# Curvature stage: where the mixed square, the cross product and the numerator stand in each engine's queue

## What is computed

```python
def step(u, _):
    ux, uy, uxx, uxy, uyy = _derivs(u)          # Sobel stencils, each clipped to -10..10
    g2 = ux * ux + uy * uy
    denK = jnp.maximum(1.0 + g2, EPS)
    K = jnp.clip((uxx * uyy - uxy * uxy) / (denK * denK + EPS), -5.0, 5.0)
    denH = jnp.sqrt(1.0 + g2 + EPS)
    H = ((1.0 + uy * uy) * uxx - 2.0 * ux * uy * uxy + (1.0 + ux * ux) * uyy) / (2.0 * denH ** 3 + EPS)
    H = jnp.clip(H, -5.0, 5.0)
    diff = jnp.clip(alpha * K + beta * H, -1.0, 1.0)
    u = u + DT * diff
    u = jnp.pad(u[:, :, 1:-1, 1:-1], ((0, 0), (0, 0), (1, 1), (1, 1)), mode='edge')
    return (u, None)
u, _ = jax.lax.scan(step, x, None, length=TIME_STEPS)
return 0.7 * u + 0.3 * x
```

## Time and profile before

| what | value |
|---|---|
| runs | 766.85, 767.97 and 768.89 us, median 767.97 |
| profiled execution | 767.58 us, its span 765.8 us |
| mean granted TensorE clock | 0.951 |
| busy share of the span | TensorE 87%, VectorE 57%, ScalarE 48%, GpSimd 42% |
| curvature stage | about 424 us to the end of the span |

### The profile page before, as it was taken

The page is one execution under the profiler, slowest core; times in us unless marked ns, Lnnn a source line. Parts: engine busy times, 40 slices in busy tenths (PEclk is TensorE's granted clock), DMA queues, the critical chain, the costliest instruction groups (busy, mean ns, idle before and its releaser), DMA issues.

```text
span 765.8 us, 11096 instructions
## 1 busy us (share of the span) xinstructions
PE 666.3 (87%) x4344; PEld 462.5 (60%) x4344; DVE 437.4 (57%) x642; ACT 371.2 (48%) x620; POOL 324.5 (42%) x311
## 2 busy tenths in 40 slices
PE   5997898999975556688998879999999999999994
PEld 4773774565442223444464768777777878777782
DVE  5630000095041012222434469999999999999997
ACT  1310000060000001110223469999999999999995
POOL 1000000010032400000001469999999999999993
PEclk9999999999995779999999979999999999999997
DMA  9999999999999999999962000000000000000001
GB/s 340 432 406 403 407 419 413 428 421 409 424 401 391 419 427 424 431 427 423 426 274 93 1 0 1 0 0 0 0 0 0 0 0 0 0 0 0 0 0 55
DMA packets 20945, 166.52 MB, mean 217 GB/s; under 512 B 1840, under 2 KB 2224, under 8 KB 11568
## 3 DMA queue, kind: packets, MB, share of 16 engines
q1 hardware_dynamic: 19552, 162.60, 51.5%
q0 software_dynamic: 688, 2.04, 0.8%
q10 hardware_dynamic: 672, 1.41, 0.5%
HBM read 164.99 MB, written 1.05 MB: 217 GB/s over the span
## 4 chain that ended last, share of the span: by engine, by line
DVE 33%; DMA 28%; PE 25%; issue 7%; ACT 4%; POOL 2%; DVEq 0%; POOLq 0%; SPq 0%; ACTq 0%
DMA ring<-wout_w 15%; PE bank L373 6%; DVE ring L863 6%; PE bank L389 5%; DVE ring L868 5%; DVE ring L850 4%; PE bank L523 4%; PE bank L442 4%; PE bank L497 4%; DMA ring<-wv_p 4%; DVE bank L847 3%; DVE bank L883 3%; DMA ring<-wv_w 3%; DMA ring<-wqk_p 3%; DMA ring<-wout_p 3%
## 5 line engine op out<-in xcount | busy, mean ns | idle before, releaser
L574 PE MATMUL bank<-u_parts,vmr 128*128 128x480 f32 x1360 | 313.4, 388 | 13.2 <-DVE ring L863 6.3
L574 PEld LDWEIGHTS bank<-u_parts,vmr 128*128 128x128 f32 x1360 | 253.1, 190 | 73.7 <-DVE reg_a L857 15.4
L389 PE MATMUL bank<-ring,small 128*32 128x256 f32 x1152 | 79.5, 424 | 36.2 <-DMA ring<-wout_w 32.3
L389 PEld LDWEIGHTS bank<-ring,small 128*32 128x32 f32 x1152 | 39.3, 119 | 69.6 <-issue 30.3
L389 PE MATMUL bank<-ring,xw 128*32 128x256 f32 x1024 | 63.9, 410 | 15.8 <-DMA ring<-wv_w 15.8
L1086 POOL MEMSET reg_d<- 128x2176 f32 x1 | 1.9, 1916 | 151.8 <-PE bank L449 151.8
L1114 POOL DMA_DIRECT2D vmr<-vmats x1 | 0.6, 566 | 148.0 <-PE bank L389 148.0
L702 DVE SCALAR_TENSOR_TENSOR reg_a<-bank,prm 128x512 f32<-128x512 f32 x4 | 2.8, 692 | 105.7 <-PE bank L449 105.7
L373 PE MATMUL bank<-reg_a,ring 128*128 128x256 f32 x256 | 57.9, 388 | 3.4 <-DMA ring<-wqk_p 2.6
L389 PEld LDWEIGHTS bank<-ring,xw 128*32 128x32 f32 x1024 | 34.0, 117 | 44.0 <-DMA ring<-wv_w 19.5
L994 ACT ACTIVATE reg_e<-xa 32x384 f32<-32x384 f32 (+7 forms) x20 | 9.1, 457 | 98.3 <-DVE xa L831 72.1
(11 more groups left out here) (195 smaller groups left out, 1008.0 us busy)
## 6 DMA issues: line engine op xcount, KB each, us to landing
ring<-wv_w SPq DMA_DIRECT2D x32, 2048.0 KB, 24.0
ring<-wout_w SPq DMA_DIRECT2D x30, 2048.0 KB, 36.7
ring<-wqk_p SPq DMA_DIRECT2D x4, 2048.0 KB, 20.1
ring<-wqk_w SPq DMA_DIRECT2D x4, 2048.0 KB, 21.9
ring<-wv_p SPq DMA_DIRECT2D x2, 2048.0 KB, 22.9
ring<-wout_p SPq DMA_DIRECT2D x2, 2048.0 KB, 22.5
ring<-wout_w SPq DMA_DIRECT2D x4, 1024.0 KB, 36.0
vmr<-vmats POOLq DMA_DIRECT2D x1, 1664.0 KB, 7.2
```

The lines of the kernel that those rows point to most:

```text
L389: ins = te.matmul(bank[32 * j:32 * j + 32, b_, n0:n0 + 256], lhs(c), slot[k % NSLOT][:, c, 256 * j:256 * j + 256], start=start and c == 0, ...
L574: last = te.matmul(dst[:, 0:NF], mat(m, first), p3[:, 2 + off:S + off, :], start=(high and n == 0), stop=(not high and n == len(terms) - 1))
```

## The change

VectorE issues `clipxy` behind `outer`, and `cross` directly behind it; `diff` of k-1 comes after both, and so directly ahead of `clipd` of k-1 in the next slot. `cross` no longer waits for `sqxy`. ScalarE issues `sqxy` between `lnd` and `inv`, and it now waits for `cross` instead of `clipxy`; `hi` moves behind `inv`. GpSimd issues `num` of k-1 in slot k, behind `hn` of k-1 and ahead of `cxy`; `pad` moves ahead of `lo`. No instruction is added or taken away.

```diff
@@ VectorE
-                    v.wait_ge(pe["fldxy"], k)
-                    v.tensor_scalar(mixed(q), mixed(q), 10.0, -10.0, ALU.min, ALU.max).then_inc(ve["clipxy"], 1)
-
                     v.wait_ge(ac["sqr"], k)
                     v.scalar_tensor_tensor(slope[q], fields_in(q, 1)[:, 0, :], 1.0, p2[q],
                                            ALU.add, ALU.add).then_inc(ve["slope"], 1)
...
                     v.scalar_tensor_tensor(two(ab[q]), fields_in(q, 0, 2), 1.0, two(f(q, 3, 2)),
                                            ALU.add, ALU.mult).then_inc(ve["outer"], 1)
+
+                    v.wait_ge(pe["fldxy"], k)
+                    v.tensor_scalar(mixed(q), mixed(q), 10.0, -10.0, ALU.min, ALU.max).then_inc(ve["clipxy"], 1)
+
+                    v.wait_ge(po["cxy"], k)
+                    v.wait_ge(ve["clipxy"], k)
+                    v.scalar_tensor_tensor(cxy[q], cxy[q], -2.0, mixed(q), ALU.mult, ALU.mult).then_inc(ve["cross"], 1)
                 if old:
 
                     v.wait_ge(ac["ends"], k - 1)
                     v.scalar_tensor_tensor(mixed(n), end_k[n], ten_ab[:, 0:1], mixed(n),
                                            ALU.min, ALU.add).then_inc(ve["diff"], 1)
-                if new:
-
-                    v.wait_ge(po["cxy"], k)
-                    v.wait_ge(ve["clipxy"], k)
-                    v.wait_ge(ac["sqxy"], k)
-                    v.scalar_tensor_tensor(cxy[q], cxy[q], -2.0, mixed(q), ALU.mult, ALU.mult).then_inc(ve["cross"], 1)
@@ ScalarE
                 if new:
-                    a.wait_ge(ve["clipxy"], k)
-                    a.activation(sqm[q], fields_in(q, 2)[:, 0, :], ACT.Square).then_inc(ac["sqxy"], 1)
                     a.wait_ge(ve["slope"], k)
                     a.activation(lnw[q], slope[q], ACT.Ln, bias=D_EPS).then_inc(ac["lnw"], 1)
...
                     a.activation(den[q], den[q], ACT.Ln, bias=D_EPS).then_inc(ac["lnd"], 1)
-                if c is not None:
-                    high(k + 2, c, not first or k + 2 > NCH)
+                    a.wait_ge(ve["cross"], k)
+                    a.activation(sqm[q], fields_in(q, 2)[:, 0, :], ACT.Square).then_inc(ac["sqxy"], 1)
...
                              scale=-1.0).then_inc(ac["inv"], 1)
+                if c is not None:
+                    high(k + 2, c, not first or k + 2 > NCH)
@@ GpSimd
                     p.tensor_tensor(num[n][:, NF:2 * NF], abs_[n], cxy[n], ALU.add).then_inc(po["hn"], 1)
+                    p.wait_ge(po["m"], k - 1)
+                    p.wait_ge(ac["sqxy"], k - 1)
+                    p.tensor_tensor(num[n][:, 0:NF], mxy[n], sqm[n], ALU.subtract).then_inc(po["num"], 1)
...
+                if border is not None:
+                    p.wait_ge(ve["u"], k - 2)
+                    inner = u3(border)[:, 2:S:S - 3, :]
+                    p.tensor_tensor(u3(border)[:, 1:S + 1:S - 1, :], inner, ones[:, 0:2 * B].rearrange("p (x b) -> p x b", x=2), ALU.mult).then_inc(po["pad"], 1)
                 if c is not None:
                     low(k + 1 if later else k + 2, c, later)
...
-                if border is not None:
-                    p.wait_ge(ve["u"], k - 2)
-                    inner = u3(border)[:, 2:S:S - 3, :]
-                    p.tensor_tensor(u3(border)[:, 1:S + 1:S - 1, :], inner, ones[:, 0:2 * B].rearrange("p (x b) -> p x b", x=2), ALU.mult).then_inc(po["pad"], 1)
-                if new:
-                    p.wait_ge(po["m"], k)
-                    p.wait_ge(ac["sqxy"], k)
-                    p.tensor_tensor(num[q][:, 0:NF], mxy[q], sqm[q], ALU.subtract).then_inc(po["num"], 1)
```

## The result

The changed kernel takes 775.52 us (median; 774.01 to 778.51), the kernel before 768.43 beside it. The ratio is 1.010, 95% interval 1.0065 to 1.0135: slower, by 7.1 us. All ratios compare undisturbed executions; one of the four of experiment 3 took 3643.36 us and is left out of its figures.

What follows compares the result with a forecast made beforehand. ScalarE's own queue was taken as the bound at 7.905 us a slot, VectorE 0.13 below; afterwards VectorE at 8.10. Terms 6.4, 0.77, 0.3, 0.33 and 0.17 sum to 8.0 on 767.58, giving 775.6 us, range 772 to 778.5.

Steps and rivals of the forecast that it cites:

- the two dependent neighbours: On VectorE, `cross` behind `clipxy` adds 0.19 and `clipd` behind `diff` 0.14 a slot, taking 7.77 to 8.10 us.
- the ring of `inv`, `kh` and `up_h`: Waits between ScalarE and VectorE, the alternative holder of 7.905 us; the change would cut it by 0.52.
- The first rival: On VectorE, a dependent neighbour costs nothing; only the ramp is left, 768.4 us, no change; chance 0.10.
- the rule cited for it: Trainium skill page on VectorE: next operation waits until the pipe empties, so a semaphore between neighbours costs nothing extra.
- faster: A ring through ScalarE held 7.905 and dependences are free, so VectorE's 7.77 is next: 763.2 us; chance 0.03.
- ramp, to `kh` of step 5: In the first steps, `hi` behind `inv` delays `kh`; with about 0.23 coming back, +0.77 us.
- TensorE's slower multiplies: After longer idle time, TensorE's field step 4 runs slowly and `clip2` comes late: 0 or 0.6, taken as 0.3 us.
- 33 slots: Steady slots from step 5 to 38 each go from 7.905 to 8.10 us: 6.4 us.
- `kh` 38 to 39: In the tail, this distance goes from 7.77 to 8.10 us: +0.33.
- `kh` 39 to 40: In the tail, this distance goes from 7.67 to the 7.86 of `num`'s path: about +0.17 us.
- the cover of `num`: On GpSimd, `num` reaches `kh` at 7.86, 0.24 us ahead of `kh` at 8.10, so its move stays hidden.
- The rival on GpSimd: GpSimd's waits for `sqxy` and `outer` add, closing the loop later than VectorE: slot 8.25, 780.6 us; chance 0.09.

Runs made afterwards that it cites:

- experiment 3: The changed kernel with `hi` issued ahead of `inv` again, behind `sqxy`: 773.53, 775.36 and 775.61 us, ratio 1.0093 to the kernel before.
- Experiment 5: The changed kernel with `cross` multiplying by the square of uy instead of the clipped uxy, nothing moved: 769.44 us, ratio 1.0030 to the kernel before.
- experiment 8: The kernel of experiment 7 with `cross` issued ahead of `diff`, so `diff` stands directly ahead of `clipd`: 768.68 us, ratio 1.0019 to the kernel before.
- experiment 7: The kernel before with three wait pairs turned (`end_k` at `ends`, `w15` at `lnd`, `inv` at `kh`): 764.40 us, ratio 0.9958.
- experiment 6: The kernel of experiment 4 with three more wait pairs turned, at `ends`, `lnd` and `kh`: 772.33 us, ratio 1.0066 to the kernel before.
- experiment 4: The changed kernel with the two waits of `cross` in the other order, `cxy` written last: 773.52 us, ratio 1.0076 to the kernel before.
- experiment 1: The changed kernel with `clipxy` issued between `slope` and `outer`: 781.43 us, ratio 1.0176 to the kernel before.
- experiment 2: The changed kernel with VectorE in the order of before, ScalarE and GpSimd as changed: 783.09 us, ratio 1.0205 to the kernel before.
- experiment 9: The kernel of experiment 7 with `clipxy` between `slope` and `outer` and `sqxy` between `lnw` and `psq`: 781.06 us, ratio 1.0165 to the kernel before.

## Why the prediction was right

**The slot.** VectorE took over with 8.10, as worked out, from the two dependent neighbours. `clipxy` to `cross` came to the 0.75 that was taken, `diff` to `clipd` to 0.75 where slot 41 had shown 0.76, and L857 to `kh` to 0.57 for 0.56. Experiment 5 shows the first by taking the dependence away, experiment 8 the second by making it in the other kernel. That ScalarE decided the kernel before is shown by experiments 7 and 6 together: the same turns save 0.07 a slot there, and nothing where VectorE decides.

They don't tell ScalarE's own queue from the ring of `inv`, `kh` and `up_h`, since the turns shorten both. The ramp of the kernel before does. From step 3 to step 4 `up_h` comes 472.49 - 464.06 = 8.43 later, 0.53 of it for the copy `x3` (L1064), and `kh` had ended at 470.77 + 1.15 = 471.92, 0.57 ahead of `up_h`. So with no wait for `kh` the queue still takes 8.43 - 0.53 = 7.90:

```profile
464.06 0.59 ACT L1037 ACTIVATE ring<-ring 128x480 f32<-128x480 f32 x1
...
470.57 0.62 ACT L1064 ACTIVATE ring<-reg_g 128x512 f32<-128x512 f32 x1
471.10 0.59 ACT L1032 ACTIVATE ring<-ring 128x480 f32<-128x480 f32 x1
471.59 0.95 ACT L1033 ACTIVATE bank<-ring 128x960 f32<-128x960 f32 x1
472.49 0.59 ACT L1037 ACTIVATE ring<-ring 128x480 f32<-128x480 f32 x1
```

In the changed kernel it is the same: the slot of 8.10 less ScalarE's new wait of 1.08 - 0.89 = 0.19 is 7.91.

**The first rival**, that a dependent neighbour costs nothing, fell, and the rule cited for it does not hold for this pair: `clipxy` to `cross` is 0.57 without the dependence, 0.69 with it, 0.75 with the wait for it written second. The second, *faster*, fell with it, since it needed free dependences too.

**The sum against the trace.** Of the 8.0 predicted, 7.39 came between the two profiled executions.

| term | predicted | measured |
|---|---|---|
| ramp, to `kh` of step 5 | 0.77 | 53.08 - 52.54 = 0.54 |
| TensorE's slower multiplies | 0.3 | 0 in this execution |
| 33 slots | 6.4 | 33 x 0.195 = 6.4 |
| `kh` 38 to 39 | 0.33 | 8.10 - 7.77 = 0.33 |
| `kh` 39 to 40 | 0.17 | 7.74 - 7.67 = 0.07 |

The ramp is counted from `clip1` of step 1. In it `kh` 1 to 2 grew by 13.28 - 12.57 = 0.71 (forecast 0.80) and `kh` 2 to 3 by 0.21 (0.20), and `kh` 3 to 5 gave back 0.34 (0.23).

Whether the 0.3 comes depends on the execution. In that of experiment 4, TensorE took 10.29 for step 3, was idle for 2.99, began step 4 at 457.18 and was granted 0.50 from 458 to 462, and `clip2` waited 0.88 for it; in that of experiment 3 it waited 0.75. In the changed kernel's, TensorE took 9.18 for step 3, was idle for 4.09 and began step 4 at 459.80; it was granted 0.61 and 0.54 in the two stretches from 460 to 464 and 1.00 from there, and `clip2` did not wait. So the forecast's span for this term, 0 or 0.6, was too narrow above. The rows of experiment 4:

```profile
458.00:460.00 2.00, 2.00 (x6) 0.50 0.01 4
460.00:462.00 2.00, 2.00 (x6) 0.50 0.00 0
462.00:464.00 2.00, 2.00 (x8) 0.66 0.02 4
```

(length, TensorE busy and its multiplies, granted clock.) Two us of full-speed work hold 10 or 11 multiplies, these hold 6.

**What the prediction left out.** It said "`hn` waits for `cross`" and put the cover of `num` at 0.24. `num` ended 0.33 ahead of `kh`, and where `kh` does wait for it (experiments 1 and 2) it starts 0.03 behind it and not 0.09, so the cover was 0.30. That is also part of why `kh` 39 to 40, which does hang on `num`, grew by 0.07 and not 0.17. But `hn` waits for `absum` as much as for `cross`, and `absum` for `outer`. The rival on GpSimd named the right engine, with `outer` as a wait of `absum`, but dismissed it path by path with that path missing. It did no harm to the forecast, because the change puts `outer` 0.57 earlier (2.69 behind `kh` for 3.26); it did spoil the expectations of experiments 1 and 9.

**The total.** The forecast of 775.6 lies within 0.1 of the measured median, and that is luck in part. The forecast added 8.0 to an execution of 767.58; the medians rose by 7.1, from 768.43. The sum was 0.9 too large and its base 0.85 too low. The profiled execution was 3 us slower than the median, and its front part took 3.39 longer than that of the kernel before; what the forecast rests on, the stage, is what the table compares.

## What to carry to other kernels

When several in-order engines are all near full, a step moved next to its producer costs the overlap of two instructions plus the wait, 0.12 to 0.19 us here, in every round, and the profile shows no idle time for it: read start-to-start distances. Before moving a step on one engine, follow every ring that closes on the product it feeds, each wait of each member, the engine's own earlier results too. And where an instruction waits for two results, try both orders of the waits; three pairs turned gave 0.4% in the kernel before.

## What was not expected

The order of two waits in front of one instruction has a price: 0.75 against 0.69 on VectorE (`cross`), 0.87 against 0.81 and 0.68 against 0.62 on ScalarE (`ends`, `lnd`). At `kh` of step 5, which waits for `inv` in both, it is 0.12 behind the end of `inv` in the kernel before and 0.09 in experiment 7. The wait written last shows in the chain as a piece of the queue of its own (DVEq L882, 0.02, with 0.03 and 0.04 around it), and in these cases the fast order is the one in which the result that comes last is waited for in the first line. Each was seen with the other result already there; what the order costs when both come together was not tried.
